# Batch 0's scatter slots made first, and fifteen tiles of layer 2 moved between two chunks of layer 1

## The reference, cut to what matters

```python
x = x + gnn(layernorm(x), edges, ew)          # two layers, below
x = x + experts(layernorm(x))                 # top 2 of 8 per token
x = x + recurrent(layernorm(x), edges, ew)    # 5 steps, each a sum over edges and a GRU cell
x = x + second_ffn(layernorm(x))
# gnn, each of its two layers:
ew  = clip(abs(edge_weight), 1e-6);  deg = segment_sum(ew, col) + 1;  dis = rsqrt(deg)
agg = segment_sum((dis[row] * ew * dis[col])[:, None] * (h @ W)[row], col)
h   = relu(layernorm(agg + dis * dis * (h @ W) + b)) + h
```

## Time and profile before

| | |
|---|---|
| runs (median of 3) | 3534.27 us (3533.43 to 3535.15) |
| profiled execution, its own time | 3545.46 us |
| span of the profile | 3543.9 us |
| busy share PE / DVE / ACT / POOL | 85% / 59% / 44% / 40% |
| granted PE clock, mean | 0.891 |
| POOL, line 563 | 1292.7 us in 784 scatters |
| PE, line 685, recurrent layer | 1943.1 us in three groups of 1750 products |

### The profile page before, as it was taken

One profiled execution on the slowest core, in us unless ns is written; L12 is line 12 of the kernel. 1 busy time (PEld: TensorE's weight loads), 2 busy tenths in 40 slices (PEclk: granted clock), 3 DMA queues, 4 the chain that ended last, 5 costly groups with the idle time before them and its releaser, 6 DMA issues.

```text
span 3543.9 us, 50941 instructions
## 1 busy us (share of the span) xinstructions
PE 2995.1 (85%) x16716; PEld 2695.2 (76%) x16717; DVE 2107.8 (59%) x4637; ACT 1565.2 (44%) x3207; POOL 1418.6 (40%) x934
## 2 busy tenths in 40 slices
PE   4661346975999499995998999999999999999898
PEld 2561345865788399995897899989988998899777
DVE  6892786754778666667454555455555554555556
ACT  3861565422455133334443444444444444444355
POOL 2688888887888366667885000000000000000000
PEclk9555556987999699997999999999999999999799
DMA  9997998645866534527654333343334333333110
GB/s 305 383 324 208 282 303 215 165 103 96 224 166 138 184 102 141 149 34 195 162 131 104 126 117 130 117 134 124 129 117 139 125 123 116 127 130 104 41 39 25
DMA packets 411194, 538.62 MB, mean 152 GB/s; under 512 B 149539, under 2 KB 307018, under 8 KB 410762
## 3 DMA queue, kind: packets, MB, share of 16 engines
q1 hardware_dynamic: 275668, 484.49, 41.0%
q0 software_dynamic: 118944, 18.55, 8.9%
q10 hardware_dynamic: 16406, 33.30, 2.6%
HBM read 398.99 MB, written 137.25 MB: 151 GB/s over the span
## 4 chain that ended last, share of the span: by engine, by line
PE 58%; POOL 13%; DVE 5%; issue 4%; DMA 2%; ACT 1%; SPq 0%; POOLq 0%; ACTq 0%; DVEq 0%
PE bank L685 54%; POOL plane_w L563 7%; POOL plane_a L563 6%; PE bank L787 1%; DMA gring_lo<-plane_a 1%; PE bank L699 1%; PE bank L864 1%; DMA plane_a<-pair,slot 0%; DVE ring_lo L1870 0%; DMA plane_w<-pair,slot 0%; PE bank L779 0%; ACT ring_hi L1241 0%; DVE gates_sb L1896 0%; PE bank L928 0%; POOLq L556 0%
## 5 line engine op out<-in xcount | busy, mean ns | idle before, releaser
L563 POOL DMA_INDIRECT plane_a<-pair,slot x392 | 636.9, 1625 | 204.5 <-issue 113.6
L563 POOL DMA_INDIRECT plane_w<-pair,slot x392 | 655.8, 1673 | 132.1 <-issue 120.2
L685 PE MATMUL bank<-ring_hi,h_hi 128*128 128x448 f32 x1750 | 654.3, 374 | 55.3 <-DVE ring_lo L1870 49.9
L1241 ACT ACTIVATE ring_hi<-ring_lo 128x448 fp32r<-128x448 f32 x875 | 496.9, 576 | 397.9 <-PE bank L685 376.5
L1870 DVE TENSOR_TENSOR ring_lo<-ring_lo,ring_hi 128x448 fp32r<-128x448 f32 x875 | 523.1, 621 | 241.9 <-ACT ring_hi L1241 241.2
L685 PE MATMUL bank<-ring_lo,h_hi 128*128 128x448 f32 x1750 | 644.6, 368 | 0.0
L685 PE MATMUL bank<-ring_hi,h_lo 128*128 128x448 f32 x1750 | 644.2, 368 | 0.0
L614 POOL DMA_DIRECT2D v_lo<-gru_v x4 | 3.0, 754 | 1083.9 <-PE bank L685 1083.9
L685 PEld LDWEIGHTS bank<-ring_hi,h_hi 128*128 128x128 f32 x1750 | 331.8, 190 | 84.8 <-DVE h_lo L1937 37.4
L1888 DVE SCALAR_TENSOR_TENSOR gates_sb<-bank,bhh,gates_sb 128x448 f32<-128x448 f32 x70 | 47.9, 684 | 520.5 <-ACT gates_sb L1265 520.5
L685 PEld LDWEIGHTS bank<-ring_hi,h_lo 128*128 128x128 f32 x1750 | 331.5, 189 | 28.4
(11 more groups left out here) (386 smaller groups left out, 6376.2 us busy)
## 6 DMA issues: line engine op xcount, KB each, us to landing
ring_lo<-plane_w SPq DMA_DIRECT2D x175, 1120.0 KB, 5.4
gring_lo<-plane_a SPq DMA_DIRECT2D x50, 1280.0 KB, 6.0
plane_w<-nat SPq DMA_DIRECT2D x100, 400.0 KB
plane_a<-nat SPq DMA_DIRECT2D x75, 448.0 KB
w_hl<-w_split SPq DMA_DIRECT2D x16, 2048.0 KB
xT<-in_L_ffn_W SPq DMA_DIRECT2D x32, 512.0 KB, 7.2
w_split<-xT SPq DMA_DIRECT2D x32, 512.0 KB, 3.2
w_split<-nat SPq DMA_DIRECT2D x32, 512.0 KB, 4.6
```

Source lines behind the costliest of these rows:

```text
L563: g_.indirect_dma_start(out=plane, out_offset=bass.IndirectOffsetOnAxis(slot[:, t:t + 1], 0), in_=pair[:, k, t:t + 1], in_offset=None, com ...
L685: last = mm(ps, lhs[x], rhs[y], start=start and n == 0, stop=stop and n == 2)
L1241: A(ring_hi[:, t % HS, :], ring_lo[:, t, :].bitcast(FP32), ACT.Copy).then_inc(hi_rdy, 1)
```

## The change

1. The start. PE's order becomes sums of batch 0, products 0, products 1, sums of batch 1, products 2, sums of batches 2 and 3, products 3. On ACT the copy of batch 0's sums comes right behind the marks of batch 0, ahead of `keep_v(0)`. On DVE `place(0, 0)` comes ahead of `compare(1, 1, 0)`.
2. The list of chunk groups is written out (`GROUPS`), and SP, PE, ACT and DVE follow it. It has q = 0 to 4; the first three groups (15 tiles) of q = 7; q = 5 and 6; then the fourth group of q = 7, the first of q = 8, the last of q = 7, and the rest of q = 8; then q = 9 to 13.
3. q = 5 and q = 6 sum in the same PSUM pair, as q = 7 holds the other; a chunk waits for the copy of the last chunk in its pair.
4. The end steps of a chunk come at tiles that `after` gives. Those of q = 4 go over the 15 tiles of q = 7 and on into q = 5; the copy of q = 5 comes at its own last tile; those of q = 6 go over ten tiles from tile 15 of q = 7 on, those of q = 7 over the rest of q = 8.

```diff
+RG = NT // RB
+AHEAD, SPLIT = 3, 1
+GROUPS = [(q, r) for q in range(5) for r in range(RG)] + [(7, r) for r in range(AHEAD)] + [(q, r) for q in (5, 6) for r in range(RG)] + [(7, 3), (8, 0), (7, 4)] + [(8, r) for r in range(SPLIT, RG)] + [(q, r) for q in range(9, 2 * GCH) for r in range(RG)]
+TILES = [(q, RB * r + i) for q, r in GROUPS for i in range(RB)]
+AT = {x: n for n, x in enumerate(TILES)}
+DONE = [AT[(q, NT - 1)] + 1 for q in range(2 * GCH)]
+PAIR = [0 if q in (5, 6) else q % 2 for q in range(2 * GCH)]
+LAST_IN_PAIR = {q: max([p for p in range(2 * GCH) if PAIR[p] == PAIR[q] and DONE[p] <= AT[(q, 0)]], default=-1) for q in range(2 * GCH)}
+def after(q, t):
+    if q == 4:
+        return AT[(7, 0)] + t
+    if q == 5 and t == 1:
+        return DONE[5] - 1
+    if q == 6:
+        return AT[(7, 15)] + t * 9 // 18
+    if q == 7:
+        return AT[(8, RB)] + t * 19 // 23
+    return AT.get((q + 1, t), len(TILES))
+def chunk_due(n, t):
+    return next((q for q in range(2 * GCH - 1) if after(q, t) == n), None)
...
@@ SP
-            for q in range(2 * GCH):
+            for n, (q, r) in enumerate(GROUPS):
...
-                if q == GCH:
-                    sp.wait_ge(used, NT * GCH)
+                if (q, r) == (GCH, RG - 1):
+                    sp.wait_ge(used, DONE[GCH - 1])
@@ PE
-            pe.wait_ge(vw_in, 16 * (1 + LAYERS))
-            products_v(0)
...
+            sum_batch(0, 0)
+            pe.wait_ge(vw_in, 16 * (1 + LAYERS))
+            products_v(0)
             products_v(1)
-            for i in range(2):
-                for b in range(2):
-                    sum_batch(2 * i + b, b)
-                products_v(2 + i)
+            sum_batch(1, 1)
+            products_v(2)
+            for b in range(2):
+                sum_batch(2 + b, b)
+            products_v(3)
...
-                if q >= 2:
-                    pe.wait_ge(aggT_rdy, q - 1)
+                if t == 0 and LAST_IN_PAIR[q] >= 0:
+                    pe.wait_ge(aggT_rdy, LAST_IN_PAIR[q] + 1)
...
-                    if t == MID and q > 0:
-                        project(q - 1)
+                due = chunk_due(n, MID)
+                if due is not None:
+                    project(due)
@@ ACT
-            keep_v(0)
-            keep_v(1)
...
-            marks(0, 0)
+            take_sums(0, 0)
+            keep_v(0)
+            keep_v(1)
+            load_keys(KB, 0)
+            mark_low(1, 1)
...
@@ DVE
+            place(0, 0)
             compare(1, 1, 0)
-            place(0, 0)
```

More of the change, by code:

```diff
@@ L399, in _ @@
             sp.wait_ge(prepared, LIMITS)
-            for q in range(2 * GCH):
+            for n, (q, r) in enumerate(GROUPS):
                 c = q % GCH
-                if q < GCH:
+                if q < GCH and r == 0:
                     landed = sp.value_load(landed_by[0:1, c:c + 1], min_val=LANDED, max_val=LANDED * NB)
@@ L406, in _ @@
                     hold(sp)
-                if q == GCH:
+                if q == GCH + 1 and r == 0:
                     for h in range(2):
                         sp.wait_ge(scat_a[h], LANDED * NB)
[L410 to L416, removed]
-                    sp.wait_ge(used, NT * GCH)
+                if n >= RP:
+                    sp.wait_ge(used, RB * (n - RP + 1))
+                sp.dma_start(gring_lo[:, RB * (n % RP):RB * (n % RP + 1), 0:GWID[c]].bitcast(FP32),
+                             adj_a[RB * r * 128:RB * (r + 1) * 128, GOFF[c]:GOFF[c] + GWID[c]].rearrange("(b p) d -> p b d", p=128)).then_inc(ring_in[n % RP], 16)
+                if (q, r) == (GCH, RG - 1):
+                    sp.wait_ge(used, DONE[GCH - 1])
                     sp.dma_start(nat[:, 0:NT - 1, :], x_tiles).then_inc(x_in, 16)
@@ L1124, in take_agg @@
                 for f in range(KD):
-                    last = A(aggT[:, f, 0:w_], sum_ps[q % 2][f][:, 0:w_], ACT.Copy)
+                    last = A(aggT[:, f, 0:w_], sum_ps[PAIR[q]][f][:, 0:w_], ACT.Copy)
                 last.then_inc(aggT_rdy, 1)
@@ L1161, in _ @@
                 high_a(n)
[L1162 to L1176, removed]
+            for n, (q, t) in enumerate(TILES):
+                if n + RH < len(TILES):
+                    high_a(n + RH)
+                due = chunk_due(n, 1)
+                if due is not None:
+                    take_agg(due)
+                if t == TN and q >= GCH + 2:
+                    normal_tokens(q - 2)
+                due = chunk_due(n, MID + 8)
+                if due is not None:
+                    chunk_root(due)
+                if t == TT + 1 and q >= GCH + 2:
+                    keep_tokens(q - 2)
+                due = chunk_due(n, MID + 18)
+                if due is not None and due >= GCH:
+                    token_roots(due)
             take_agg(2 * GCH - 1)
@@ L1670, in _ @@
                 low_a(n)
[L1671 to L1694, removed]
+            for n, (q, t) in enumerate(TILES):
+                if n + RL < len(TILES):
+                    low_a(n + RL)
+                due = chunk_due(n, MID + 1)
+                if due is not None:
+                    take_conv(due)
+                due = chunk_due(n, MID + 3)
+                if due is not None:
+                    keep_finite(due)
+                due = chunk_due(n, MID + 6)
+                if due is not None:
+                    spread(due)
+                due = chunk_due(n, MID + 9)
+                if due is not None:
+                    normalize(due)
+                due = chunk_due(n, MID + 12)
+                if due is not None:
+                    add_to_res(due)
+                due = chunk_due(n, MID + 15)
+                if due is not None and due < GCH:
+                    scale_again(due)
+                if due is not None and due >= GCH:
+                    add_input(due)
+                due = chunk_due(n, MID + 19)
+                if due is not None and due >= GCH:
+                    token_scales(due)
+                if t == TG + 1 and q >= GCH + 2:
+                    take_logits(q - 2)
             last_q = 2 * GCH - 1
```

40 lines of the change are left out of this document (19 added, 21 removed).

## The result

| | kernel before | changed kernel |
|---|---|---|
| median of 20 runs each | 3536.39 us | 3512.34 us |
| ratio, 95% interval | | 0.9932 (0.9919 to 0.9946) |
| span of the profiled execution | 3543.9 us | 3515.3 us |
| first scatter into plane_a | 77.00 | 67.28 |
| last scatter into plane_a | 850.46 | 849.02 |

The change is worth 24.05 us (19.1 to 28.6); 23.9 was forecast, as 3510 us. In the two traces the gather comes 20.6 us earlier, and the profiles differ by 28.5 at their ends. The other 8 us arise in the recurrent layer, where nothing was changed.

The account below looks back on a forecast made before the run. PE and POOL were taken to set the end by turns, via the experts' start. Terms -9.0 + 1.6 + 2.7 - 20.4 + 1.2 = -23.9 us gave 3521.6 profiled; runs' median, 11.2 lower, 3510 us, in 3503 to 3517 (wider range 3502 to 3525).

Parts of the forecast that it names:

- the start: Batch 0's sums, copy and slots go first, so POOL's first scatter comes at 68.0 instead of 77.00: 9.0 us gained.
- the tiles: Fifteen layer 2 tiles fill PE's 39 us gap before chunk 5, taking 20.4 us off layer 2.
- the tail: Behind chunk 6, PE waits 3.3 us at tile 23 of q = 7 and an old 2.14 us wait goes: net +1.2 us.
- The hand-over: Chunk 6 shares chunk 5's PSUM pair and waits for ACT's copy of chunk 5's sums: PE starts it 2.7 us later.
- I keep the whole 9.0: After the first scatter, POOL loses none of the start's 9.0 us gain, as later batches don't wait for slots.
- landings: Rival: early half batches land slower under SP's fills; at 18 us each, seven cost 5 us apiece, giving 3545; chance 0.07.
- What the tiles cost POOL: Scatters beside the tiles' loads take 0.13 us longer, 12 of them, so chunks 5 and 6 land 1.6 us later.
- Batch 1's slots: Rival: batch 1's slots come late, with 1.4 us of slack, and at worst the start's 9.0 us is lost: 3519; chance 0.13.
- chunk 4's steps within chunk 5: Chunk 4's last DVE steps delay chunk 5 by about 5 us, costed at nothing since the wait for chunk 6's data hides it.

Follow-up runs that it names:

- the reload runs: Changed kernel with the reload of x two groups later (ratio 0.9944) or one later (0.9952), and all_three with it one later (0.9930), each against the kernel before.
- copy_first: Changed kernel with chunk 5's sums copied out of PSUM on ACT ahead of the seven roundings of chunk 6's tiles; ratio 0.9942 against the kernel before.
- twenty_in_time: Changed kernel with 20 layer 2 tiles ahead, chunk 4's split ahead of chunk 5's, chunk 6's sums copied before later roundings; ratio 0.9917 against the kernel before.
- start_only: Kernel before with only the start's edits (batch 0's sums, copy and slots first), no tiles ahead, no shared PSUM pair; ratio 0.9985 against the kernel before.
- one_product_first: Changed kernel with one of the two recurrent products ahead of batch 0's sums, the other behind; ratio 0.9935 against the kernel before.
- all_three: twenty_in_time with the edits of copy_first and one_product_first added; ratio 0.9915 against the kernel before.

## Why the prediction was right, and where it was not

**The total** was right: 24.05 us measured, 23.9 forecast. The trace up to the gather gives 20.6, so the sum was 3.3 too high by it; the runs' interval (19.1 to 28.6) holds both, and that the medians meet the forecast within 0.2 us is luck. In the trace the start and POOL's terms gave 4.0 in place of 7.4, the tiles and the tail together 20.1 in place of 19.2, and 0.7 us went between layer 2's end and the gather. plane_w's last scatter came at 1899.5, 18.5 us earlier, where 1894 was forecast.

**The tiles** (20.4 forecast) were right in mechanism and size. From chunk 6's start to layer 2's end it is 259.46 us, 279.54 before: 20.1 us less, where -20.4 + 1.2 was forecast. The tail was mis-sized: 1.15 us of wait at tile 23, not 3.3, beside 1.5 at chunk 6's projection in the group ahead of it. The load of the next group came sooner than the 12.04 us that I took (9.2 from issue to rounding). That it stands behind x is what the reload runs show: 5.9 us without x ahead, 12.2 with. By the Trainium skill's "DMA: Bandwidth & Descriptors", section Queues, rings and completion order, a ring is worked off in order; these times agree.

**The hand-over** (+2.7) was exact: 7.0 us from issue to start became 9.7, and copy_first took 2.2 of it back.

**The start** was right where it was worked out (9.7, forecast 9.0) and wrong in "I keep the whole 9.0". The rival "landings" took a small part: 1.6 us here, 0.9 to 3.8 in the other runs with the early start, on the two half batches that wait at all, not seven.

**What the tiles cost POOL** (+1.6) is the step that failed. The prediction named its own test, plane_a's last scatter at least 6 us earlier; it came 1.4 us earlier. The 0.13 us a scatter from the earlier trace rows were put down to loads. But the first of the two stretches had the more DMA traffic, and in the second only the scatters beside DVE's splits were longer. It is DVE's work that holds a scatter: 6.5 us over the last 56, where 1.6 were forecast. Between 792 and 831 DVE had been idle, and the tiles fill just that. Some of it came back at the landing: chunk 6's loads were issued 7.6 us after the last scatter's start, 10.1 before. So at chunk 6's issue 4.0 us of the start were left, where 7.4 were forecast.

By the Trainium skill's "SBUF — State Buffer", section Who interferes with whom, a VectorE instruction with two SBUF inputs contends with a GpSimd instruction that reads SBUF. The splits have two such inputs, and the rows agree that a scatter waits. By the Trainium skill's "SBUF — State Buffer", section SBUF: two separate sides, the pair of ports that they share is locked for the length of an instruction. One instruction of 3.49 us did hold a scatter (4.49 us, twenty_in_time), but one was also held through nine in a row.

**Batch 1's slots** were not late, and **chunk 4's steps within chunk 5** cost PE nothing that lasted. Chunk 5's tiles took 31.0 us; before it was 32.6, and 33.7 in start_only, both with a projection of 3.6 among them, so the steps took some 1 to 2 us, not 5. PE waited 8.65 us for chunk 6 behind them in any case. They cost POOL what is said above: a step "hidden" from the queue that waits for it was not hidden from another.

What stays open: the shorter landing was not tested by itself, nor a scatter beside splits with all else the same. The 1.42 us are a pattern of 14 traces, and which scatter is held is not known.

## What to carry to other kernels

Work put into an idle gap is free only if every engine that it wakes is free to others there: list what ran undisturbed in the gap, GpSimd's DMA issues too. Before a step is moved, read for each engine what stands ahead of it in the list and which load that waits for; twice here a copy or split of a chunk already done stood behind work that waited for a load still to come. Where a change of 0.7% is the matter, compare landmarks ahead of the stretch that varies from execution to execution.

## What the runs showed of the hardware

- A scatter's issue on GpSimd, 1.55 us alone, took 3.8 to 5.9 us beside an unbroken run of five to nine VectorE splits, and in 30 of 31 cases ended 1.42 us behind the run. Beside one two-input VectorE instruction of 3.49 or 1.64 us it took 2.9 to 4.5 us, with the same 1.42 us in 12 cases of 12. Other scatters beside such runs took 1.55 to 2.1 us.
- A granted clock of 1.00 in a row by windows can mean that the trace has no record of the clock there. Changed kernel, window over batch 0's degree products:

```profile
57.80:63.70 5.90, 5.90 (x32) 5.90 (x30) 0.00 (x0) 0.00 (x0) 0.00 (x0) 1.00 1.03 411
```

The 28 products took 6.15 us, as at 0.50 (1.2 GHz) in the earlier trace rows, after 14.2 us of idle PE ahead of the sums. This trace's first clock record, of 1.00, begins at 69.53 us; the row's 1.00 is no reading. Where records cover the sums they agree with the durations: 3.29 us in one_product_first, within a record of 1.00 but for the last 0.1 us, and 4.48 in all_three, where the clock fell midway.
- The recurrent layer's same matmuls took 1650 to 1666 us in different executions.
